# Attention of 16 heads in pairs: stacked score operands of contraction 128, copied by DMA, and another order of work on each engine

## The reference

```
q = einsum('qdh,bcd->bhcq', Q, x) * sq          # 16 heads, 64 wide
k = einsum('qdh,bcd->bhcq', K, x) * sq
v = einsum('vdh,bcd->bhcv', V, x) * sv
att = einsum('bhcq,bhCq->bhcC', q, k) / d_query ; causal mask
p = softmax(att)
y = einsum('bhcC,bhCv->bhcv', p, v)
z = einsum('dvh,bhcv->bcd', W, y) * ...          # added to x
```

## Time and profile before

| what | us |
|---|---|
| median of three runs | 1520.9 |
| the profiled execution | 1514.62 |
| its span | 1512.6 |
| attention a | about 66 to 242 |
| experts, first | about 242 to 414 |
| attention b | about 414 to 1322 |
| experts, second | about 1322 to 1512 |

### The profile page before, as it was taken

How to read it: one execution, slowest core, us unless ns; L and a number is a source line. 1 busy time by engine, 2 the same in 40 slices (tenths; PEclk the granted TensorE clock), 3 DMA queues, 4 the chain that set the end, 5 groups by cost and what they waited for, 6 DMA issues and landing times. The chain is left out here.

```text
span 1512.6 us, 28432 instructions
## 1 busy us (share of the span) xinstructions
PE 1302.4 (86%) x8377; PEld 1111.3 (73%) x8377; DVE 1100.1 (73%) x2826; ACT 941.5 (62%) x2522; POOL 760.4 (50%) x950
## 2 busy tenths in 40 slices
PE   1587635999669999999999999999999998299992
PEld 1476534999648888888888888888888886199991
DVE  5666544777548888888887887888888887277773
ACT  1554422444348878888788888888787886054440
POOL 3005563444325555576575675665765665434443
PEclk9986657999869999999999999999999999599996
DMA  9391011222100000000000000000000000022215
GB/s 181 125 375 36 29 39 50 61 59 62 29 30 11 2 15 1 1 26 5 3 24 5 4 26 1 22 8 1 8 8 1 12 5 4 29 61 62 60 52 172
DMA packets 91936, 64.47 MB, mean 43 GB/s; under 512 B 34020, under 2 KB 77935, under 8 KB 91792
## 3 DMA queue, kind: packets, MB, share of 16 engines
q1 hardware_dynamic: 78928, 43.65, 10.8%
q0 software_dynamic: 8640, 16.93, 3.5%
q10 hardware_dynamic: 4224, 2.10, 0.5%
HBM read 26.59 MB, written 36.96 MB: 42 GB/s over the span
## 5 line engine op out<-in xcount | busy, mean ns | idle before, releaser
L1366 POOL TENSOR_TENSOR b_probs<-b_probs,b_recip 128x128 f32<-128x128 f32 (+3 forms) x512 | 352.7, 719 | 307.2 <-DVE b_recip L1599 307.2
L420 DVE TENSOR_TENSOR b_pt_lo<-b_ring,b_pt_hi 128x512 fp32r<-128x512 f32 (+1 forms) x384 | 219.1, 598 | 93.1 <-ACT b_pt_hi L414 87.8
L545 ACT ACTIVATE b_probs<-b_s_bank,b_neg_max 128x256 f32<-128x256 f32 (+3 forms) x512 | 267.9, 533 | 27.7 <-DVE b_neg_max L537 26.3
L537 DVE TENSOR_REDUCE b_neg_max<-b_s_bank 128x1 f32<-128x256 f32 (+3 forms) x512 | 219.7, 479 | 47.8 <-PE b_s_bank L529 46.8
L1227 POOL DMA_INDIRECT y_rows<-f_y_sb,f_dest x142 | 139.1, 979 | 192.7 <-DVE f_y_sb L1200 185.0
L414 ACT ACTIVATE b_pt_hi<-b_ring 128x512 fp32r<-128x512 f32 (+1 forms) x384 | 192.2, 547 | 9.5 <-PE b_ring L485 8.6
L485 PE MATMUL b_ring<-ident,b_probs 128*128 128x128 f32 x1280 | 179.3, 278 | 4.8 <-DVE b_q_lo L420 4.8
L81 PE MATMUL b_s_bank<-b_k_hi,b_q_hi 64*128 64x256 f32 (+3 forms) x512 | 180.6, 353 | 2.9 <-ACT b_probs L545 1.4
L1170 ACT ACTIVATE f_hid_hi<-f_hid_bank 128x384 fp32r<-128x384 f32 x142 | 69.9, 492 | 160.1 <-PE f_hid_bank L1123 142.1
L82 PE MATMUL b_s_bank<-b_k_lo,b_q_hi 64*128 64x256 f32 (+3 forms) x512 | 164.4, 321 | 0.0
L83 PE MATMUL b_s_bank<-b_k_hi,b_q_lo 64*128 64x256 f32 (+3 forms) x512 | 163.8, 320 | 0.0
(11 more groups left out here) (304 smaller groups left out, 3345.2 us busy)
## 6 DMA issues: line engine op xcount, KB each, us to landing
x_sorted<-a_blank SPq DMA_DIRECT2D x64, 260.0 KB, 3.9
f_xs<-x_sorted SPq DMA_DIRECT2D x142, 65.0 KB
b_yc<-y_rows SPq DMA_DIRECT2D x16, 256.0 KB, 3.2
f_yc<-y_rows SPq DMA_DIRECT2D x16, 256.0 KB, 5.1
y_rows<-f_y_sb,f_dest POOLq DMA_INDIRECT x142
x_tok<-in_L_attn_a_x_dram SPq DMA_DIRECT2D x8, 256.0 KB, 4.6
out_dram<-x_tok ACTq DMA_DIRECT2D x8, 256.0 KB, 5.3
f_raw<-in_L_ffn_W_dram SPq DMA_DIRECT2D x1, 1408.0 KB, 6.7
```

The lines of the kernel that those rows point to most:

```text
L420: nc.vector.tensor_tensor(dst, src(rg.of(key)), hi.bitcast(F32), ALU.subtract).then_inc(rg.lo_done, 1)
L537: nc.vector.tensor_reduce(sc.neg_max[:, i:i + 1], s_tile(sc, i), AX.X, ALU.max, negate=True).then_inc(sc.max_done, 1)
L545: nc.scalar.activation(probs[:, P_AT[i]:P_AT[i] + (i + 1) * P], s_tile(sc, i), ACT.Exp, bias=sc.neg_max[:, i:i + 1], accum_out=sums[:, i:i ...
L1366: nc.gpsimd.tensor_tensor(part, part, recip[:, i:i + 1].to_broadcast([P, (i + 1) * P]), ALU.mult).then_inc(probs_done, 1)
```

## The change

In attention b the slots of one head become periods p of two heads, even = 2p and odd = 2p + 1, and each engine's loop is rewritten for a period. Scores are taken from stacked operands: for a head, `stack` holds q_hi over q_lo in its 128 rows, k_hi over k_hi, and k_lo over k_lo; two passes of contraction 128 give all four products (lo*lo too). ACT and DVE write q and k into one tile, `qk`, in the order q_hi, k_hi, k_lo, q_lo, and SP copies the 64 rows of each head from there into its stack, by three DMAs. There are two stacks, one for even and one for odd heads. PE waits for the copy instead of k's lo half; SP waits for k's lo half and for the masks of the head before; ACT and DVE wait for both copies of a pair before they write the next pair's q and k.

The score tiles are issued largest first: (3), (2), (1, 0), in attention a too. The masks of a group come later than its scores. The transposes wait for all four divisions of a head instead of the first. q and k are projected at two places of the period. Values, one bank per period, come after the first score tile. Scatters go three in a period instead of one in a slot; those of the last sequence all come after the loop. SP loads yc earlier. Some tiles share memory (z with the routing's xn_t, xn with yc[1], over with apart).

```diff
-S_GROUPS = ((1, 0), (2,), (3,))
-S_AT = {1: (0, 0), 0: (0, 2 * P), 2: (1, 0), 3: (2, 0)}
-S_READ = (2, 3, 4)
+S_GROUPS = ((3,), (2,), (1, 0))
+S_AT = {3: (0, 0), 2: (1, 0), 1: (2, 0), 0: (2, 2 * P)}
+S_READ = (1, 2, 4)
...
+        z = sb("z", [P, T], F32)
+        rt = Route(nc, ctx, "b_r", 1, pl, z)
...
-        q = (sb("q_hi", [P, T], F32R), sb("q_lo", [P, T], F32R))
-        k = (sb("k_hi", [P, T], F32R), sb("k_lo", [P, T], F32R))
+        qk = sb("qk", [P, 4, T], F32R)
+        q, k = (qk[:, 0, :], qk[:, 3, :]), (qk[:, 1, :], qk[:, 2, :])
+        stack = [sb(f"stack{i}", [P, 3, T], F32R) for i in range(2)]
+        stack_in = [sem(f"stack_in{i}") for i in range(2)]
...
+            def rows_of(b):
                 wait(sp, yc_added, b)
+                if b:
+                    ring_filled(sp, rg, ("xn", b - 1))
...
+            def stacked(u):
+                pair, half = divmod(u, 2)
+                rows = qk[half * KD:half * KD + KD].bitcast(F32)
+                to = stack[half][:].bitcast(F32)
+                sp.wait_ge(rg.lo_done, rg.lo["k", pair])
+                wait(sp, sc.s_full, (u - 1) * len(S_GROUPS))
+                sp.dma_start(to[0:KD, :, :], rows[:, 0:3, :]).then_inc(stack_in[half], 16)
+                sp.dma_start(to[KD:P, 0, :], rows[:, 3, :]).then_inc(stack_in[half], 16)
+                sp.dma_start(to[KD:P, 1:3, :], rows[:, 1:3, :]).then_inc(stack_in[half], 16)
+
+            rows_of(0)
+            for u in range(NU):
+                stacked(u)
+                if u == 0:
+                    rows_of(1)
+                b, h = divmod(u, NH)
+                if h == 2 * TURNED + 2 and b + 2 < NB:
+                    rows_of(b + 2)
...
+            def divide(u):
+                pool.wait_ge(recip_done, u + 1)
+                for i in range(QT):
+                    part = probs[u % 2][:, P_AT[i]:P_AT[i] + (i + 1) * P]
+                    nc.gpsimd.tensor_tensor(part, part, recip[:, i:i + 1].to_broadcast([P, (i + 1) * P]),
+                                            ALU.mult).then_inc(probs_done, 1)
+
...
+            for p in periods:
+                if paired(p - 2):
+                    y_low(p - 2)
+                if coming(p, SUMMED) is not None:
+                    summed(coming(p, SUMMED))
+                if coming(p, ADDED) is not None:
+                    rstd(nc, pool, g, n, coming(p, ADDED))
+                if leaving(p, MEANT) is not None:
+                    rstd(nc, pool, g, rt.m, leaving(p, MEANT))
+                if leaving(p, DOUBLED) is not None:
+                    route_dest(nc, pool, g, rt, leaving(p, DOUBLED))
+                if paired(p):
+                    divide(2 * p)
+                    divide(2 * p + 1)
+                sent(p)
...
             def scores(u, group):
-                if u % 2 == 0 and group == 0:
-                    pe.wait_ge(rg.lo_done, rg.lo["k", u // 2])
-                rows = slice(u % 2 * KD, u % 2 * KD + KD)
...
+                if group == 0:
+                    pe.wait_ge(stack_in[u % 2], (u // 2 + 1) * 3 * 16)
                 s_free(pe, sc, u, group)
                 for i in S_GROUPS[group]:
-                    st = [part[rows, i * P:i * P + P] for part in q]
-                    mv = [part[rows, 0:(i + 1) * P] for part in k]
-                    three_passes(nc, s_tile(sc, i), st, mv, i == S_GROUPS[group][0], False)
+                    for part in (1, 2):
+                        nc.tensor.matmul(s_tile(sc, i), stack[u % 2][:, 0, i * P:i * P + P],
+                                         stack[u % 2][:, part, 0:(i + 1) * P],
+                                         start=(i == S_GROUPS[group][0] and part == 1), stop=False)
...
+            def transposes(u):
+                if alive(u):
+                    pe.wait_ge(probs_done, u * QT + QT)
+                    for i in range(len(PT_BANKS)):
+                        head_transpose(nc, pe, rg, turns(u), probs[u % 2], i, g.ident)
...
+            for p in periods:
+                even, odd = 2 * p, 2 * p + 1
+                scores(even, 0)
+                masks((even - 1, 2), (even, 0))
+                if paired(p):
+                    values(p)
+                products(even - 3)
+                transposes(even - 2)
+                scores(even, 1)
+                scores(even, 2)
+                masks((even, 1), (even, 2))
+                if paired(p + 1):
+                    project("q", g.b_q, p + 1)
+                scores(odd, 0)
+                if paired(p + 1):
+                    project("k", g.b_k, p + 1)
+                if coming(p, TURNED) is not None:
+                    turn(coming(p, TURNED))
+                if leaving(p, Z_TURN) is not None:
+                    output_turn(leaving(p, Z_TURN))
+                if leaving(p, ROWS) is not None:
+                    route_turn(nc, pe, g, rt, rg, leaving(p, ROWS))
+                if leaving(p, SCORED) is not None:
+                    route_score(nc, pe, g, rt, rg, leaving(p, SCORED))
+                if leaving(p, COUNTED) is not None:
+                    route_count(nc, pe, g, rt, rg, leaving(p, COUNTED))
+                products(even - 2)
+                scores(odd, 1)
+                masks((odd, 0), (odd, 1))
+                transposes(odd - 2)
+                if paired(p - 2):
+                    output(p - 2)
+                scores(odd, 2)
...
+            for p in range(NU // 2 + PERIODS):
+                even, odd = 2 * p, 2 * p + 1
+                transposed(even - 2, 0)
+                transposed(even - 2, 1)
+                exponentials(even, 0)
+                if paired(p - 2):
+                    y_high(p - 2)
+                transposed(even - 2, 2)
+                exponentials(even, 1)
+                if paired(p + 1):
+                    for copied in stack_in:
+                        act.wait_ge(copied, (p + 1) * 3 * 16)
+                    split_hi(nc, act, rg, ("q", p + 1), q[0])
+                    split_hi(nc, act, rg, ("k", p + 1), k[0])
+                if coming(p, TURNED) is not None:
+                    turned(coming(p, TURNED))
+                if leaving(p, ROWS) is not None:
+                    route_turned(nc, act, g, rt, rg, leaving(p, ROWS))
+                exponentials(even, 2)
+                y_half(even - 2)
+                transposed(odd - 2, 0)
+                exponentials(odd, 0)
+                transposed(odd - 2, 1)
+                transposed(odd - 2, 2)
+                exponentials(odd, 1)
+                if paired(p + 1):
+                    values_hi(p + 1)
+                exponentials(odd, 2)
+                y_half(odd - 2)
...
+            for p in periods:
+                even, odd = 2 * p, 2 * p + 1
+                maxima(odd - 2, 2)
+                maxima(even, 0)
+                if paired(p):
+                    hi, lo, bank = v_parts(p)
+                    split_lo(nc, dve, rg, ("v", p), lo, hi, bank)
+                inverse(odd - 2)
+                y_sum(odd - 4)
+                transposed(even - 2, 0)
+                transposed(even - 2, 1)
+                maxima(even, 1)
+                transposed(even - 2, 2)
+                maxima(even, 2)
+                if paired(p + 1):
+                    for copied in stack_in:
+                        wait(dve, copied, (p + 1) * 3 * 16)
+                    split_lo(nc, dve, rg, ("q", p + 1), q[1], q[0])
+                    split_lo(nc, dve, rg, ("k", p + 1), k[1], k[0])
+                if coming(p, TURNED) is not None:
+                    turned(coming(p, TURNED))
+                if leaving(p, SCORED) is not None:
+                    route_scored(nc, dve, g, rt, rg, leaving(p, SCORED))
+                    route_rank(nc, dve, g, rt, rg, leaving(p, SCORED))
+                if leaving(p, COUNTED) is not None:
+                    route_place(nc, dve, g, rt, rg, leaving(p, COUNTED))
+                maxima(odd, 0)
+                inverse(even)
+                maxima(odd, 1)
+                transposed(odd - 2, 0)
+                y_sum(even - 2)
+                transposed(odd - 2, 1)
+                transposed(odd - 2, 2)
+                if leaving(p, Z_ADD) is not None:
+                    added(leaving(p, Z_ADD))
+                    moments(nc, dve, g, rt.m, leaving(p, MEANT), x_done, leaving(p, MEANT) + 1)
+                if leaving(p, APPLIED) is not None:
+                    shift(nc, dve, g, rt.m, leaving(p, APPLIED))
+                if coming(p, ADDED) is not None:
+                    summed(coming(p, ADDED))
+                    moments(nc, dve, g, n, coming(p, ADDED), yc_added, coming(p, ADDED) + 1)
+                if coming(p, NORMED) is not None:
+                    shift(nc, dve, g, n, coming(p, NORMED))
```

More of the change, by code:

```diff
@@ new lines, in sent @@
+            def sent(p):
+                b, i = p // PERIODS - 2, p % PERIODS
+                if 0 <= b < NB - 1 and i < SENT:
```

(27 more changed lines are left out.)

268 lines of the change are left out of this document (81 added, 187 removed).

## The result

The changed kernel takes 1727.5 us (median of four runs, 1723.8 to 1732.7), the kernel before 1519.5 in the runs beside it: a ratio of 1.137, interval 1.133 to 1.141. The change costs 208 us. The profiled execution took 1730.9, its span is 1729.2 us.

The account below looks back on a forecast made before the run. PE was taken to bound the kernel, full at 13.04 us a pair. 1514.6 + 228 for 64 pairs at 16.6 + 6 for the first copy = 1749, said as 1755 for the median; range 1490 to 1830.

Parts of the forecast that it names:

- PE's gain: Attention b scores: 12 matmuls a head become 8, saving 0.82 us a head, 1.64 a pair, 105 us in all.
- Rival D: Copies hidden altogether (L at most 2.8): 11.4 us a pair, -105 us, 1416 us; chance 0.02.
- L: Time from a head's first copy issue on SP to the last landing: 5.8 us taken, bounds 4.1 to 6.1.
- The data term: Part of L for moving 786 KB: 2.0 us at a_blank's rate, 4.05 if rate goes with partitions touched.
- The fixed term: Part of L without data: 2.1 us, taken from a 32 KB load landing 2.2 us after issue.
- Rival A: Copies move at a_blank's rate: L = 4.1, 12.7 us a pair, clock kept, 1503 us; chance 0.22.
- The ring 2L + 3.8: Attention b: even and odd copies lie one behind the other, so a pair takes 15.4 us at L = 5.8.
- the second route, ACT's queue: From masks through ACT's queue to k_lo, one copy and scores: 8.6 + L a pair, later with a short L.
- what would prove me wrong: Forecast is wrong if L is under 4.5 us, or if the even and odd copy overlap.
- The clock: PE idling 26% lowers its clock, under 0.9 in the stage: 2.4 us a pair at 0.66 throughout, half taken, 1.2.
- Smaller parts: Tile order in attention a 0 +-4; separate projections, later transposes, fewer scatters 0, up to 20 us; SP's y rows 0.
- The beginning: Attention b starts with one copy that nothing covers: 6 us.

Follow-up runs that it names:

- with the copies hidden: Changed kernel with the two moves, q and k projected one period earlier into a second q/k tile, next-sequence work one period earlier: 1519.8 us, ratio 1.0014.
- with the wait filled: Changed kernel with eight extra 512-column matmuls on PE before it waits for the even stack, result overwritten: 1706.3 us, ratio 1.123.
- with the copies made twice: Changed kernel with each head's three DMAs issued a second time after the first have landed: 2439.7 us in one run.
- With small copies: Changed kernel where, from the second pair on, each copy moves 64 of 512 columns: 1593.0 us in one run, beside 1518.3.
- The order alone: Changed kernel without stacks or copies; scores in three passes as before, two q/k tiles in turn: 1673.2 us, ratio 1.103.
- the two steps: POOL divides the even head before both layernorm waits; DVE adds z before its last transposes. Changed kernel with them 1716.0 us; order without copies with them 1591.8 us.
- The spread version: Kernel with q and k projected one period earlier, its once-per-sequence work spread over different periods: 1494.5 us, ratio 0.986 to the kernel before.

## Why the forecast was right, and where it was not

The time was forecast at 1755 and is 1727.5, slower by 208 where 234 was forecast; the pair at 16.6 and is 16.20. Step by step:

- **PE's gain, 0.82 us a head: right.** Rival D's floor of 11.4 us a pair was reached at positions 4 to 6 with the copies hidden (11.2 to 11.6).
- **L = 5.8: right, 5.6 in the kernel, 5.5 alone.** The data term was taken at the upper end, 4.05, and is 3.7 to 4.0. The fixed term was 2.1 and is 1.5 to 1.8. Rival A needed L under 4.4 and fell with this.
- **The ring 2L + 3.8: right for the pairs that keep the clock, and not the last route in most others.** With the measured copies it gives 14.6 to 14.7, and 5 of the 28 pairs in the stretch go round it, the shortest in 14.6 us; with the wait filled it is 14 of 28, and with the copies made twice all of them. In the other 23 of the changed kernel, PE reaches the odd head's scores after the copy has landed, and no copy but the even one is waited for. The forecast's paragraph on the clock had this: 7.7 us of PE's work at a lowered clock, 1.5 us past the landing. In the first pair shown it is 923.90 - 916.24 = 7.7 us, some 1.7 past a landing 5.4 us after the issue at 916.77. What it did not have is that the second route, ACT's queue, is by then about as late: ACT has its k half 0.56 us after its q half, one behind the other. With small copies, in the pair whose masks start at 1013.26, the way from the masks to the next issue is 1021.57 - 1013.26 = 8.3 us; in the first pair shown it is 10.5. Of these 2.2 us about 0.8 are masks and values at half the clock, 0.8 ACT's wait for head_pv, which is at half the clock too, and 0.6 the routing's copy in ACT's queue. The "what would prove me wrong" of the forecast, even and odd copy overlapping, didn't come about.
- **The clock: right in kind.** 0.90 in the stretch, at the bound that I gave and not under it, with PE idle for 22%. Its price was forecast as 1.2 us a pair. What the rows give is 16.20 - 14.6 = 1.6 for clock and once-per-sequence work together, and over all pairs they aren't parted; in the first pair shown about 1.6 us are the clock's and 0.6 the routing's.
- **Smaller parts at 0: wrong, and covered by luck.** GpSimd's 291 busy us of 460 were read as a queue that is never late. But what counts is what stands queued behind a wait, and there POOL stood up to 8.8 us with the divisions behind it. The order alone costs 155 us. In the changed kernel most of this lay beside the copies: moving the two steps gave 12 us back. So it hardly shows in the forecast's sum, but it is the likely reason why hiding the copies gave 1520 and not 1416.
- **The beginning: 6 forecast, 16.3 measured.** Attention b's first matmul, in the kernel before and in the changed one:

```profile
424.54 1.11 PE L1385 MATMUL b_ring<-ident,b_xn 128*128 128x128 f32 x4 [18.69 <-ACT b_xn L473]
```

```profile
428.51 1.12 PE L1414 MATMUL b_ring<-ident,b_yc 128*128 128x128 f32 x4 [18.62 <-ACT b_yc L473]
```

So 4.0 us had passed before the stage began. They aren't the copies': with the two steps moved, it begins at 424.63. The other 12.3 lie inside: from this matmul to the first y_hi it is 38.3 us before, 38.1 in the order alone (426.17 to 464.31) and 50.6 in the changed kernel. I counted one copy without cover, but the first y_hi comes in the third period, so several copies lie ahead of it.

The time came nearer than its terms. The pace was forecast at 228 us and is 199, the beginning at 6 and is 16.3; the two errors partly cancel.

What stays open: why positions 2 and 3 stay long in the order alone after the two steps were moved; the share of each of the two steps; and why position 3 takes 23.3 us in the order alone but 16.2 with copies, where the same work is queued. The spread version makes uneven queues the likely cause, since it moved nothing but that, but it changed several places at once, and no run takes them one by one.

## What to carry to other kernels

Cost a copy by what it waits for and what waits for it, follow it all round to the next copy, and work out every route, since the last one may be another than the longest on paper, and may change from pair to pair: here a loop with two copies in it was last in 5 of 28 pairs, and a queue with one in most others. Making the operands one period earlier took the copies of 5.6 us off the path almost altogether (11.4 us of waits for 169), for the price of one more tile (here a borrowed one, saved and fetched back). A step whose engine has time to spare isn't free if it begins with a wait and per-head work is queued behind it; look at the pace by position in the cycle, for a mean hides both: with small copies it is 14.1 us, over positions of 12.1 to 17.6.

## What the runs showed of the hardware

- A copy from SBUF to SBUF of 768 KB takes 5.5 us over 64 partitions and 3.5 over 128. Rows 0 to 63 and rows 64 to 127 as sources are alike (5.5 and 5.4 us a round).
- Three DMAs issued one behind the other land as one of their sum would: 5.5 us for 128 + 256 + 384 KB, 5.5 for 768 KB at once, all touching 64 partitions on one side at least.
- The issues themselves take SP 0.46, 0.60 and 1.22 us in the rows above; with 48, 32 and 16 KB each about 0.6. For the small copies this is most of what comes on top of the 2.0 us that one of 48 KB takes.
- Behind a wait of 2.80 us PE ran from 915.2 to 920.2 at a granted clock of 0.50, the level of 1.2 GHz; behind another of 2.96 us, at 833.70, it kept 1.00. At the earlier trace rows, without such waits, it kept 1.00 throughout.
